# A four-layer transformer kernel on one core: small identity products on TensorE at stage borders, ahead of loads and in the last cross-attention

## The reference

```
x = x + _L0_xattn_ref(_layernorm(x), ctx_768, ...)   # 16 heads of 64
x = x + _L0_attn_ref(_layernorm(x), ...)             # 16 heads, relative bias
x = x + _L0_ffn_ref(_layernorm(x), ...)              # weights and inputs quantised to FP4 blocks
x = x + _L1_xattn_ref(_layernorm(x), ctx_768, ...)   # scores clipped
x = x + _L1_attn_ref(_layernorm(x), ...)             # one head
x = x + _L1_ffn_ref(_layernorm(x), ...)              # low rank
x = x + _L2_xattn_ref(_layernorm(x), ctx_768, ...)   # 16 heads
x = x + _L2_attn_ref(_layernorm(x), ...)             # linear attention, a scan over tokens
x = x + _L2_ffn_ref(_layernorm(x), ...)              # experts with a capacity
x = x + _L3_xattn_ref(_layernorm(x), ctx_768, ...)   # one head over the context
x = x + _L3_attn_ref(_layernorm(x), ...)             # one head, scores through sigmoid, tanh, relu
x = x + _L3_ffn_ref(_layernorm(x), ...)              # 8 experts, top two
```

## Time and profile before

| | |
|---|---|
| median of the runs | 1909.32 us (1909.05, 1909.32, 1921.05) |
| the profiled execution | 1909.2 us |
| its span | 1907.0 us |
| TensorE busy | 1602.8 us, 84% of the span |
| VectorE busy | 1125.1 us, 59% |
| ScalarE busy | 822.1 us, 43% |
| GpSimd busy | 761.8 us, 40% |
| TensorE's mean granted clock | 0.911 |
| DMA | 213.70 MB, 112 GB/s in the mean |

### The profile page before, as it was taken

One profiled execution on the slowest core, in us unless ns is written; L12 is line 12 of the kernel. 1 busy time (PEld: TensorE's weight loads), 2 busy tenths in 40 slices (PEclk: granted clock), 3 DMA queues, 4 the chain that ended last, 5 costly groups with the idle time before them and its releaser, 6 DMA issues. The chain is left out here.

```text
span 1907.0 us, 35283 instructions
## 1 busy us (share of the span) xinstructions
PE 1602.8 (84%) x12373; PEld 1358.6 (71%) x12373; DVE 1125.1 (59%) x3117; ACT 822.1 (43%) x2394; POOL 761.8 (40%) x927
## 2 busy tenths in 40 slices
PE   6999999666868999976999999699869477739996
PEld 6899889434547999846889998646569334528995
DVE  5887876488746888644767767459721322432222
ACT  4666666113326888712666666320123022113332
POOL 6666565352329999513211111147532111030111
PEclk9999999878979999987999999999879777859998
DMA  8545543200032333206233333160152573911112
GB/s 259 178 147 179 167 150 130 76 1 1 0 120 79 129 127 137 68 19 195 95 108 106 119 107 130 69 208 1 50 184 83 137 202 116 360 45 40 40 34 86
DMA packets 139710, 213.70 MB, mean 112 GB/s; under 512 B 19450, under 2 KB 106434, under 8 KB 139058
## 3 DMA queue, kind: packets, MB, share of 16 engines
q1 hardware_dynamic: 132418, 199.50, 32.5%
q0 software_dynamic: 3408, 8.54, 1.3%
q10 hardware_dynamic: 3712, 3.41, 0.6%
HBM read 170.07 MB, written 47.78 MB: 114 GB/s over the span
## 5 line engine op out<-in xcount | busy, mean ns | idle before, releaser
L802 DVE TENSOR_SCALAR xattn_oT<-bank,xattn_last 128x256 f32<-128x256 f32 x256 | 111.7, 478 | 90.7 <-PE bank L623 90.6
L708 ACT ACTIVATE xattn_probs<-bank,xattn_negmax 128x257 f32<-128x257 f32 x256 | 123.7, 483 | 65.6 <-DVE xattn_negmax L783 65.5
L713 ACT ACTIVATE xattn_probs<-xattn_probs,xattn_rsum 128x257 f32<-128x257 f32 x256 | 131.8, 515 | 1.4 <-DVE xattn_rsum L787 1.4
L1028 POOL TENSOR_SCALAR xattn_probs<-xattn_probs,xattn_rsum 128x257 f32<-128x257 f32 x128 | 119.5, 934 | 22.8 <-DVE xattn_rsum L1263 22.8
L783 DVE TENSOR_REDUCE xattn_negmax<-bank 128x1 f32<-128x257 f32 x256 | 106.4, 416 | 34.9 <-PE bank L596 33.4
L792 DVE TENSOR_TENSOR xattn_probsT_lo<-bank,xattn_probsT_hi 128x256 fp32r<-128x256 f32 x256 | 104.9, 410 | 9.8 <-ACT xattn_probsT_hi L719 8.7
L603 PE MATMUL bank<-ident,xattn_probs 128*128 128x128 f32 x512 | 103.9, 285 | 7.1 <-ACT xattn_probs L713 6.7
L719 ACT CAST xattn_probsT_hi<-bank 128x256 fp32r<-128x256 f32 x256 | 95.4, 373 | 32.3 <-PE bank L603 28.2
L541 POOL COPY ctx_stat<-xattn_mv 128x2 f32<-128x2 f32 x32 | 6.0, 187 | 237.7 <-DVE xattn_mv L816 237.7
L592 PE MATMUL bank<-xattn_ctxT,xattn_qk_hi 128*128 128x258 f32 x256 | 93.8, 366 | 0.5 <-DVE xattn_qk L779 0.5
L2121 POOL TENSOR_TENSOR scan_product<-scan_state,scan_qT 128x512 f32<-128x512 f32 x64 | 75.6, 1182 | 36.2 <-DVE scan_state L2258 35.8
(11 more groups left out here) (503 smaller groups left out, 5297.0 us busy)
## 6 DMA issues: line engine op xcount, KB each, us to landing
xattn_ctxT<-ctx_partsT SPq DMA_DIRECT2D x64, 516.0 KB, 3.9
xattn_ctxN<-ctx_partsN SPq DMA_DIRECT2D x64, 384.0 KB, 4.4
ctx_partsT<-xattn_ctxT SPq DMA_DIRECT2D x32, 516.0 KB, 2.7
moe_w<-in_L_ffn_W SPq DMA_DIRECT2D x16, 1024.0 KB, 13.7
ctx_partsN<-xattn_ctxN SPq DMA_DIRECT2D x32, 384.0 KB, 3.6
moecap_w_early<-in_L_ffn_w SPq DMA_DIRECT2D x10, 1024.0 KB, 13.1
xattn_rawN<-in_ctx SPq DMA_DIRECT2D x32, 192.0 KB, 2.7
xattn_raw<-in_ctx SPq DMA_DIRECT2D x32, 192.0 KB, 4.4
```

The source lines that it names most:

```text
L708: nc.scalar.activation(probs[:, n % RING, :], SB[n % 2][:, 0:KV], ACT.Exp, bias=negmax[:, n % RING:n % RING + 1], accum_out=psum[:, n % RI ...
L713: nc.scalar.mul(probs[:, n % RING, :], probs[:, n % RING, :], rsum[:, n % RING:n % RING + 1]).then_inc(norm_ready, 1)
L802: nc.vector.tensor_scalar(oT[k][:, heads, b, :], by_head(OB[:, k * 2 * P:(k + 1) * 2 * P]), last[:, k, j * PER_TILE + b:j * PER_TILE + b + ...
L1028: nc.gpsimd.tensor_scalar(probs[:, n % RING, :], probs[:, n % RING, :], rsum[:, n % RING:n % RING + 1], None, ALU.mult).then_inc(norm_read ...
```

## The change

A new helper `keep_busy(n, bank)` issues n products on TensorE: the identity, read as bf16 (128 columns as the weights, 256 columns as the moving side), into 256 columns of a bank that is idle at that point. Nothing reads the result, and no semaphore is raised. It is called at 32 places in the PE functions, 1,120 products in one execution: at the front of stages (before or behind `ln.pe`, ahead of the waits for loads), in the middle of some (ahead of waits for DVE or for slots), and 8 at the end of nine stages. Three waits change. In xattn3 `scores` now waits for `scaled_ready` first, then runs 12 of them (for t of 1 and more), then waits for `T_loaded`; `turn_probs` waits for `probsT_ready`, runs 8, then waits for `probs_ready`. At the end of moe_capacity PE newly waits for the last tile's `brought` and then runs 22. The other engines' functions are as before. In the excerpts of the diff the context is cut; the line numbers behind @@ tell the place.

```diff
@@ -36,6 +36,12 @@
+    def keep_busy(self, n, bank):
+        same = self.ident[:, :].bitcast(BF16)
+        for _ in range(n):
+            self.nc.tensor.matmul(self.bank[bank][:, 0:2 * P], same[:, 0:P], same[:, 0:2 * P], start=True, stop=True)
@@ -179,6 +185,7 @@
         def _(pe):
+            core.keep_busy(34, 7)
             pe.wait_ge(loaded, 16 * LOADS)
@@ -194,6 +201,7 @@
                 mm.then_inc(y_done, 1)
+            core.keep_busy(8, 0)
@@ -651,6 +659,7 @@
+            core.keep_busy(22, 7)
             ln.pe(pe, 0)
@@ -662,6 +671,8 @@
                 j, s = divmod(t, UNITS)
+                if t == TURN and not first:
+                    core.keep_busy(22, 3)
                 if 0 <= t - TURN < ALL:
@@ -683,6 +694,7 @@
                     mm.then_inc(stat_turned, 1)
+            core.keep_busy(8, 2)
@@ -1143,6 +1155,7 @@
+            core.keep_busy(40, 7)
             for c in range(CD):
@@ -1412,7 +1427,9 @@
         def _(pe):
+            core.keep_busy(20, 7)
             ln.pe(pe)
+            core.keep_busy(40, 7)
             pe.wait_ge(loaded, 16 * LOADS)
@@ -1466,6 +1483,7 @@
                     mm.then_inc(y_done, 1)
+            core.keep_busy(8, 4)
@@ -1646,6 +1665,7 @@
             mm.then_inc(scores_done, 1)
+            core.keep_busy(38 if soft_theta else 20, 5)
             pe.wait_ge(probsT_ready, 1)
@@ -1670,6 +1690,7 @@
                     mm.then_inc(y_done, 1)
+            core.keep_busy(8, 1)
@@ -1935,6 +1956,7 @@
                 mm.then_inc(turned, 1)
+            core.keep_busy(60, 4)
             turn_x(0)
@@ -2123,7 +2146,9 @@
         def _(pe):
+            core.keep_busy(20, 7)
             ln.pe(pe)
+            core.keep_busy(45, 7)
             pe.wait_ge(loaded, 16 * 8)
@@ -2573,12 +2598,16 @@
         def _(pe):
+            core.keep_busy(20, 7)
             ln.pe(pe)
                 pe.wait_ge(ln.xnT_ready, CD * (h + 1))
+                core.keep_busy(6, 6)
                 gate.pe(pe, h)
             for h in range(2):
+                core.keep_busy(32 if h == 0 else 24, 0)
                 gate.rank(pe, h, RANK[h])
+            core.keep_busy(20, 0)
@@ -2633,12 +2662,16 @@
                     up(n)
+                if n == 0:
+                    core.keep_busy(45, 6)
                 if n + 1 < E:
                     down(n - 1)
+            pe.wait_ge(brought[TILES - 1], TOP * 16)
+            core.keep_busy(22, 0)
@@ -2894,10 +2927,13 @@
         def _(pe):
+            core.keep_busy(20, 7)
             ln.pe(pe)
+            core.keep_busy(34, 5)
             pe.wait_ge(ln.xnT_ready, 2 * CD)
+            core.keep_busy(70, 0)
             pe.wait_ge(loaded, 96)
@@ -2950,6 +2986,7 @@
             pe.wait_ge(ew.loaded, E * 32)
+            core.keep_busy(140, 0)
             turn_x(0)
@@ -3245,9 +3282,11 @@
                 pe.wait_ge(qk_ready, 2 * (t // 4 + 1))
-                pe.wait_ge(T_loaded[z], (t // RING + 1) * 48)
                 if t >= 2:
                     pe.wait_ge(scaled_ready, t - 1)
+                if t >= 1:
+                    core.keep_busy(12, t % 2)
+                pe.wait_ge(T_loaded[z], (t // RING + 1) * 48)
                 for b in range(PER_TILE):
@@ -3255,9 +3294,10 @@
             def turn_probs(t):
-                pe.wait_ge(probs_ready, t + 1)
                 if t:
                     pe.wait_ge(probsT_ready, 2 * t)
+                core.keep_busy(8, 2)
+                pe.wait_ge(probs_ready, t + 1)
                 for c in range(KCH):
@@ -3312,6 +3352,7 @@
+            core.keep_busy(16, 7)
             ln.pe(pe, 0)
```

## The result

The changed kernel takes 1925.5 us in the median of 15 executions (1916.1 to 1940.5), the kernel before 1913.1 in the same job (15 executions, 1901.0 to 1921.1): 1.0068 times as long, with a 95% interval of 1.0049 to 1.0086. That is 13 us slower, where 10 us faster was forecast. The executions scatter by some 20 us in both kernels, and part of what follows is about that scatter.

What follows compares the result with a forecast made beforehand. TensorE's mean clock of 0.911 put 339 us at 1.2 GHz, falling behind PE's idle times and costing only where PE's work is on the path. The terms sum to -9.9: 1909.3 - 9.9 = 1899.4 us, range 1884 to 1912.

Steps and rivals of the forecast that it cites:

- small ones together: Fillers at xattn0's front, xattn2's TURN, attn3 and fp4 gain -1.0, -1.3, -1.0 and -0.7: -4.0 us in all.
- gate and rank: In moe_capacity, 6 + 6 + 32 fillers where PE has no gap lengthen the path: +4.5 us, ends +1.3 and +9.5.
- last moe's -3.2: Fillers in the last moe's idle times speed up gate, rank and first slot products: -3.2 us, ends -5 and +6.
- attn0, +4.3: 40 fillers queued behind attn0's transposes delay the projections: 6.0 us less 1.7 from the clock, so +4.3.
- Borders: 8 fillers at stage ends finish 0.4 us behind DVE's last add in each of seven stages: +2.8 us.
- moe_capacity's end: 22 fillers behind the new wait for the last tile's rows end 2.4 us behind DVE: +2.4, ends 0 and +4.
- attn1: 20 fillers between scores and the wait for probsT fit into idle and speed the products behind: -2.4 us.
- low rank: 34 fillers before the load take 3.7 of 5.70 us idle; L184, sixteen transposes and first outputs halve: -3.1 us.
- xattn3, -8.3: Fillers and moved waits in xattn3's loop (scores, turn_probs) keep the clock high, shortening its iterations: -8.3 us.
- three rivals: Clock held throughout, 1882 us (0.25); low clock stays in xattn3's loop, 1924.7 (0.07); nothing that counts, 1909 +- 3 (0.13).
- rival 2: The low clock stays in xattn3's loop (scores, turn_probs): +17 in place of -8.3, 1924.7 us; chance 0.07.
- scan, -2.1: 45 fillers before scan's load take 5.0 of 6.66 us idle; L2135's 14 products run at the high level: -2.1 us.

Runs made afterwards that it cites:

- r1: The changed kernel run again, nothing altered: 1914.6 us in one execution.
- e4: Changed kernel without fillers at xattn0's start, attn0's 40, moe_capacity's gate, rank, dispatch and end, last moe's 70 and 140, all stage ends: 1896.4 us, 0.9939 times before.
- e9: e4 with 512-column fillers in the last moe (30 in place of 34 ahead of the gate, 36 behind it, 70 ahead of the slots): 1897.5 us, 0.9915 times before.
- r3: The changed kernel run again, in one job with a profile of the kernel before: 1924.1 us in one execution.
- e5: Kernel before with only the change's hunks of scores and turn_probs in xattn3's loop: 0.9975 times before.
- e8: Kernel before with only the fillers e4 leaves out, the 20 at attn0's and moe_capacity's starts, and xattn3's changed wait order: 1.0111 times before.
- r2: The changed kernel run again, nothing altered: 1.0097 times before.
- e3: Changed kernel with 70 products of 512 columns in place of the 140 fillers ahead of the last moe's slots: 1.0019 times before.
- e3b: Changed kernel with 70 products of 512 columns in place of the last moe's 140, run again: 1922.9 us in one execution.
- e6: Changed kernel with 420 fillers of 256 columns in place of the 140 ahead of the last moe's slots: 1951.6 us in one execution.
- e7: Changed kernel with 210 fillers of 512 columns in place of the 140 ahead of the last moe's slots: 1942.4 us in one execution.
- e1: Changed kernel without the 140 fillers ahead of the last moe's wait for its slots: 1917.5 us, 1.0055 times before.
- b1: A second profile of the kernel before, nothing altered: 1921.9 us in one execution.

## Why the prediction was wrong

The steps that failed, in short: "small ones together" took the first wait behind the fillers in xattn0 and xattn2 for the only one (-2.3 forecast, +5.7 in r1, of which 0.8 is the borders); "gate and rank" was paid with about 8 in place of 4.5; the last moe's -3.2 was 0.0 at best; and the hold-up of PE had no term. Then the terms one by one.

**Right in place, off in size.** *attn0, +4.3:* 40 fillers ran from 370.42, right behind the transposes, to 377.1.

```profile
369.08 1.54 PE L136 MATMUL bank<-ident,xn 128*128 128x128 f32 x6 [2.91 <-DVE xn L112]
370.42 6.71 PE L44 MATMUL bank<-ident 128*128 128x256 bf16 x40
376.96 1.88 PE L1441 MATMUL bank<-xnT,attn_w 128*128 128x512 f32 x4
```

6.71 for 40 where 6.0 was taken, and little given back: 4.1 to 6.1 with the border, against 4.7. e4 and e9, without them, are at +0.2 and -0.3. *Borders and moe_capacity's end* were right (xattn1's border, before):

```profile
816.44 1.04 PE L44 MATMUL bank<-ident 128*128 128x256 bf16 x8
```

```profile
816.64 0.42 DVE L1287 TENSOR_TENSOR x<-x,bank 128x256 f32<-128x256 f32 x1 [8.25 <-PE bank L1155]
```

PE ends 0.4 behind DVE here as forecast, and 2.5 at the end of moe_capacity. *attn1 -3.2 for -2.4, low rank -1.2 to -1.9 for -2.7:*

```profile
848.24 2.36 PE L44 MATMUL bank<-ident 128*128 128x256 bf16 x20
851.55 1.13 PE L1675 MATMUL bank<-attn_v,attn_probsT 128*128 128x256 f32 x4 [0.95 <-DVE attn_probsT L1749]
...
863.13 1.12 PE L191 MATMUL bank<-lowrank_cT,lowrank_vT 32*128 32x256 f32 x4 [0.83 <-DMA lowrank_b<-in_L_ffn_b]
864.18 1.97 PE L136 MATMUL bank<-ident,xn 128*128 128x128 f32 x16
```

16 transposes and L184 (now L191) ran at half the old price. Low rank gave less since PE still waited 0.83 for the load, which came 0.4 later in the stage than before. *xattn3, -8.3:* -6.4 to -6.7 in three profiles and -4.0 in r3, and -5.4 alone (e5); how much of that is the fillers' is uncertain by e8's -6.7 without them.

```profile
1558.78 0.87 PE L3318 MATMUL bank<-xattn_N,xattn_probsT 128*32 128x194 f32 x16
...
1571.32 1.11 PE L3292 MATMUL bank<-xattn_T,xattn_qk 128*32 128x257 f32 x8 [4.57 <-DMA xattn_T<-ctx_rows]
```

```profile
1580.00:1590.00 10.00, 9.91 (x91) 6.66 (x92) 3.24 (x10) 3.93 (x9) 0.32 (x2) 1.00 0.80 221
```

PV at 0.87, and fully busy at 1.00 where before ten us were at 0.50. One iteration still fell, behind 4.57 of idle for a load: the fillers of `scores` end well ahead of what PE waits for, and nothing refills the gap.

**Failed: the rank and gate of moe_capacity, +4.5.** It was 7.6 to 8.1 in seven profiles (the changed kernel, r1, r2, e3, e3b, e6, e7), 5.7 in e8, and 1.1 and 0.7 where the clock happened to be up (e1, r3). The step said that the gate may give back up to 3.5. In the seven it took 3.42 a half, hardly less than before, its own 12 fillers made its end 1.9 to 2.2 later, and the 32 added some 6 us.

**Failed: "small ones together, -4.0", in xattn0 and xattn2.** The sign was wrong: +1.6 to +3.3 and +1.2 to +3.4 (xattn0 is at +2.9 in b1 too, by its tail; its front is read from the rows). xattn0's front, PE before, and after:

```profile
21.52 2.95 PE L574 MATMUL bank<-xattn_qT,xattn_wk 64*128 64x128 f32 x48 [1.16 <-ACT xnT L140]
26.10 0.36 PE L592 MATMUL bank<-xattn_ctxT,xattn_qk_hi 128*128 128x258 f32 x1 [0.26 <-DVE xattn_qk L779]
```

```profile
21.34 6.38 PE L582 MATMUL bank<-xattn_qT,xattn_wk 64*128 64x128 f32 x64 [3.46 <-DMA xattn_wk<-in_L_xattn_Wk_T]
27.65 0.39 PE L600 MATMUL bank<-xattn_ctxT,xattn_qk_hi 128*128 128x258 f32 x1
```

The first 32 projections (L564) took 3.81 in place of 5.42 behind the 22 fillers, PE was ready 2.5 us sooner, and then waited 3.46 for the load of `xattn_wk`, which nothing had sped up. Behind this new wait the clock fell, and 64 products cost 6.4 where 48 and 16 had cost 4.1 of PE: unit one is 1.5 us later. All eleven profiles with these 22 show a low stretch that begins between 19.9 and 22.4 us; none of the five without does. I had taken the wait behind the fillers to be the one before them.

In xattn2 the same step failed. The 4.03 of idle in the earlier trace rows is put down to ACT, but ACT waited for DVE, and DVE for a load. DVE before, then DVE and PE after:

```profile
903.50 0.36 DVE L811 BATCH_NORM_STATS2 xattn_stats<-xattn_raw 128x6 f32<-128x192 f32 x1 [5.43 <-DMA xattn_raw<-in_ctx]
```

```profile
903.88 0.36 DVE L823 BATCH_NORM_STATS2 xattn_stats<-xattn_raw 128x6 f32<-128x192 f32 x1 [8.88 <-DMA xattn_raw<-in_ctx]
897.98 2.56 PE L44 MATMUL bank<-ident 128*128 128x256 bf16 x22
905.62 0.69 PE L611 MATMUL bank<-ident,xattn_probs 128*128 128x128 f32 x2 [5.07 <-ACT xattn_probs L725]
```

The fillers ahead of the stage brought PE to its first scores 3.4 us sooner (16.7 us into the stage, before 20.1). But the load came 28.5 us into the stage in both, so the 3.4 were waited away, the 22 fillers at `TURN` ended 5.07 ahead of the next work, and that work ran low all the same (its scores 0.21 apart). At the ninth unit of scores PE was 0.9 us later in the stage than before (41.8, before 40.9). The load came at 27.9 to 29.2 us in all sixteen profiles. How much of the 0.9 is the 22 fillers' is not shown: e8, without them, has a low stretch as long there.

The tail of xattn2 fell too, 13 us ahead of the stage's end (before, then after, the same instructions):

```profile
1214.00:1224.00 10.00, 7.17 (x83) 6.08 (x84) 1.08 (x3) 1.64 (x3) 0.00 (x0) 1.00 0.05 11
```

```profile
1216.80:1226.80 10.00, 7.52 (x75) 6.01 (x75) 0.88 (x2) 1.65 (x3) 0.00 (x0) 0.83 0.05 11
```

Neither has a filler there. The low stretch is in nine of the twelve profiles with fillers in xattn2's front (not in e4, r2, e3b) and in none of the four without. A like stretch in the tail of xattn0 came up in the first profile of the changed kernel, in e3b, in e9, and in b1, which is the kernel before. So the same idle times let the clock fall in some executions and not in others; that the fillers make it likelier is suggested by the counts and not shown.

**Failed: the last moe, -3.2.** It was 0.0 in r1, where nothing was held up, and +5.7 to +7.9 where PE was. -1.8 for the gate came in one of four profiles of the changed kernel; L2320 took 7.00 in the first. What went with it is how long PE idled between the 34 fillers and the gate: 4.3 to 4.8 us for the gate where that was 0.4 to 1.8 (e9, e3, r1), 6.4 to 7.0 where it was 3.3 to 4.2 (the nine others with fillers there). The step counted the fillers' length against the idle time, not the idle left behind them. And 140 fillers cost the path 8 us when they run in driblets.

**Not in the list at all: the hold-up while GpSimd scatters.** Against r1, which has none, the first profile is 6.2 us longer in moe_capacity and 7.9 in the last moe, which is about the distance between its 18.6 and r1's 5.3. None of the three rivals names it, and rival 2, the slower one, had its place wrong: the kernel with the loop's fillers alone (e5) was faster.

**Failed: scan, -2.1.** -0.1 to -2.6. In the first profile:

```profile
1245.60 16.80 PE L2160 MATMUL bank<-xnT,scan_w 128*128 128x512 f32 x35 [2.78 <-DMA scan_wo<-in_L_attn_out_w_T]
```

PE was ready and the clock was up, but `scan_wo` came 3.60 us later in the run than before, while the stage had begun only 3.2 later: the load is where the gain ended.

**Sum** over r1, the profile without a hold-up: +5.3, where -9.9 was forecast. Of the 15.2, xattn0 and xattn2 make 7.2, moe_capacity 3.1, the last moe 3.2, xattn3 1.9, scan 1.6 and low rank 1.5; the others give 3.2 back. The hold-ups come on top. Terms of 1 or 2 us in this list are within what one profile can differ from the next.

The Trainium skill ("TensorE: Matmul & The Clock Gate", Part 1, "What's actually happening") puts the cost of the ramp under 1% of a typical kernel. The best version here gained 0.85% (e9), which keeps within it as a bound, though the mean clock shows many falls and not one ramp. Part 4 of the same page of the Trainium skill ("PE-mode transpose") says that transposes don't count as work for the clock as products do: in low rank the sixteen ran at the high price behind 34 fillers, and at the low price before (1.97 and 3.67 us), which fits, but no run here has transposes alone in the fillers' place.

## What to carry to other kernels

A filler is worth its place only where it ends ahead of what the engine waits for at the low price too, and close enough to it that no idle is left behind it; where the engine has no wait, it is plain added time (attn0 4, rank 8 us of the path). Follow the wait that comes after the one you fill: in xattn0 the work got there earlier and waited longer, and the clock fell again. Leave loads out of the expected gain. Wide fillers hold the engine as long with half the instructions, and only narrow ones showed the gaps here; that they are better on the whole is not shown. The half of this change that comes closest to these rules makes the kernel 12 to 16 us faster (e4, e9), the other half 21 slower (e8).

## What was not expected of the hardware

In three of five jobs TensorE is held up while GpSimd issues indirect scatters: in moe_capacity's dispatch 5.4 to 11.5 us with fillers in the kernel (0.3 and 1.8 in the kernel before), and in the 140 narrow fillers 8 or 9 gaps that sum to 6.4 to 6.7 us. 70 products of 512 columns ran through it without a gap in two profiles. The chip alone does not decide: the runs of the two jobs without it and of the last job with it all have the same chip number, 4. What holds it up stays open: the fetches of instructions seen in the trace lie near it in some profiles and not in others. And one and the same kernel varies by about 20 us between executions: the clock falls in some and not in others at the same instructions (tail of xattn0, b1 against before: 2.9 us).
